# Inverse map of a mixture-of-experts layer: fp16 one-hots without tile-offset columns, each choice in its own PSUM columns

## The reference, cut to what matters

```python
x = hidden_states.reshape(-1, 256)                 # 2048 tokens
probs = softmax(x @ gate_w.T)                      # 64 experts
topk_w, topk_idx = top_k(probs, 6)
topk_w = topk_w / sum(topk_w)
h = silu(einsum('th,eih->tei', x, experts_w1))     # only the chosen experts count
y = einsum('tei,ehi->teh', h, experts_w2)
routed_out = sum over the 6 choices of topk_w * y[token, chosen expert]
out = layernorm(x + routed_out + shared_expert(x))
```

## Time and profile before

| | |
|---|---|
| median of 3 runs | 1412.85 us |
| the three runs | 1412.85, 1413.84, 1405.2 us |
| profiled execution, its own time | 1411.82 us |
| profiled execution, span from first to last instruction | 1410.1 us |
| mean granted TensorE clock | 0.894 |
| busy: PE, DVE, ACT, POOL | 1142.8, 874.5, 592.1, 568.6 us |

### The profile page before, as it was taken

One profiled execution on the slowest core, in us unless ns is written; L12 is line 12 of the kernel. 1 busy time (PEld: TensorE's weight loads), 2 busy tenths in 40 slices (PEclk: granted clock), 3 DMA queues, 4 the chain that ended last, 5 costly groups with the idle time before them and its releaser, 6 DMA issues. The chain is left out here.

```text
span 1410.1 us, 20915 instructions
## 1 busy us (share of the span) xinstructions
PE 1142.8 (81%) x6217; PEld 643.9 (46%) x6217; DVE 874.5 (62%) x1722; ACT 592.1 (42%) x1210; POOL 568.6 (40%) x565
## 2 busy tenths in 40 slices
PE   5599999999999778998898532869999889994673
PEld 2242222222222244665555431248888678882332
DVE  6499999999999366646455558943333222221656
ACT  1127777777777725450334200025555444430000
POOL 6001637765453737763110102544445754550000
PEclk9789999999999989999999755569999999997876
DMA  4970522441400130000000010058888888876411
GB/s 133 184 163 9 91 35 33 57 53 16 53 14 10 26 140 1 1 1 1 0 1 1 1 62 0 0 144 236 247 230 248 244 244 249 263 243 213 149 50 45
DMA packets 128366, 137.18 MB, mean 97 GB/s; under 512 B 47414, under 2 KB 99350, under 8 KB 128191
## 3 DMA queue, kind: packets, MB, share of 16 engines
q1 hardware_dynamic: 118767, 110.42, 31.7%
q0 software_dynamic: 9216, 25.18, 5.6%
q10 hardware_dynamic: 272, 0.26, 0.1%
HBM read 109.06 MB, written 24.12 MB: 94 GB/s over the span
## 5 line engine op out<-in xcount | busy, mean ns | idle before, releaser
L495 ACT ACTIVATE l_ret_store<-attn_st 128x512 f32<-128x512 f32 x512 | 280.1, 599 | 102.7 <-PE attn_st L406 92.8
L519 DVE TENSOR_REDUCE attn_neg<-attn_mx 128x8 f32<-128x1024 f32 x256 | 299.1, 1202 | 12.4 <-PE attn_mx L386 11.4
L1842 DVE SCALAR_TENSOR_TENSOR exp_sums<-exp_y_ps,moe_mask,exp_sums 128x256 f32 x159 | 77.0, 484 | 210.0 <-PE exp_y_ps L1776 101.6
L1767 PE MATMUL exp_h_ps<-exp_xt,exp_w 128*88 128x128 f32 x1272 | 169.8, 277 | 10.7 <-DMA exp_w<-in_w 9.7
L406 PE MATMUL attn_st<-attn_q_st,attn_k_st 128*128 128x512 bf16 x512 | 173.9, 384 | 3.0 <-ACT l_ret_store L495 2.1
L386 PE MATMUL attn_mx<-attn_k_st,attn_q_st 96*128 96x512 bf16 x512 | 155.8, 386 | 14.4 <-DVE attn_neg L519 13.9
L1776 PE MATMUL exp_y_ps<-exp_w,exp_ht 96*128 96x256 f32 x636 | 163.4, 379 | 0.0
L1767 PEld LDWEIGHTS exp_h_ps<-exp_xt,exp_w 128*88 128x88 f32 x1272 | 147.5, 158 | 29.0 <-DMA exp_w<-in_w 25.1
L418 PE MATMUL attn_o<-l_ret_store,l_ret_tab 128*32 128x512 f32 x1024 | 136.4, 605 | 0.8 <-ACT l_ret_store L495 0.8
L1726 POOL DMA_INDIRECT exp_rows<-x_rows,moe_tok_i x96 | 91.6, 954 | 90.3 <-PE exp_xt_ps L1756 68.1
L1731 POOL DMA_INDIRECT y_rows<-exp_sums,moe_dst_i x96 | 93.6, 975 | 81.2 <-DVE exp_sums L1842 73.0
(11 more groups left out here) (266 smaller groups left out, 1839.1 us busy)
## 6 DMA issues: line engine op xcount, KB each, us to landing
exp_w<-in_w SPq DMA_DIRECT2D x318, 176.0 KB
comb_got<-y_rows SPq DMA_DIRECT2D x16, 768.0 KB, 5.9
parts<-l0b_front SPq DMA_DIRECT2D x32, 192.0 KB, 10.8
attn_k_st<-parts SPq DMA_DIRECT2D x48, 128.0 KB, 7.2
attn_q_st<-parts SPq DMA_DIRECT2D x48, 128.0 KB, 7.8
l_ret_tab<-in_tables SPq DMA_DIRECT2D x4, 1024.0 KB, 11.0
keep_x_t<-in_x_t SPq DMA_DIRECT2D x4, 512.0 KB
keep_x<-in_x SPq DMA_DIRECT2D x1, 2048.0 KB, 14.7
```

The costliest lines, as they stand in the source:

```text
L495: act.activation(probs[s % 2][:, h], st_ps[n % BANKS][:], ACT.Exp, scale=SCALE0).then_inc(exp_done, 1)
L519: dve.tensor_reduce(neg[m % 2][:, i], mx_ps[slot["score", n] % 2][:].rearrange("p (j k) -> p j k", k=P), AX.X, ALU.max, negate=True).then_ ...
L1767: mm = pe.matmul(h_ps[b % 2][0:HALF, j * P:(j + 1) * P], w1[n][:, k, j], xt[b % XB][:, 0, k], start=(k == 0), stop=(k == KT - 1))
L1842: dve.scalar_tensor_tensor(out=sums[:, bass.ds(at, 1)], in0=y_ps[b % 2][:, 0:E].unsqueeze(1), scalar=mask[:, b:b + 1], in1=sums[:, bass.ds ...
```

## The change

- The 96 pairs now have one `hot_high` each, over the 96 tiles and not the 160 steps, times the token's number plus one (`token`). It and `hot_low` are fp16 and not bf16.
- Each choice `k` sums into its own 96 columns: five in `m_ps` (cleared by a product with zeros, 480 columns), the sixth in `t_ps`.
- After the loop no turning is needed: the sum over the choices is the token, and which choice's columns are not zero gives `k`. The row of `y_rows` is now k * 2048 + token, where it was (t * 8 + k) * 128 + lane.
- `mask` no longer comes from the loop's result: ahead of the loop DVE works out the first and last slot of each step's expert in its tile (`bound`), spreads them over a diagonal (`spread`), PE broadcasts them (`b_ps`), and after the loop's last one-hot DVE compares them with the lane.
- Four more constants on POOL at the start of the block; `combine` reads `y_rows` by the new layout (a line of SP).

```diff
-Y_ROWS = NT * KPAD * P
+Y_ROWS = TOP * TOK
-        hot_low = sb("hot_low", [P, HOTS, P], BF16)
-        hot_high = sb("hot_high", [P, HOTS, 2, TILES], BF16)
+        hot_low = sb("hot_low", [P, HOTS, P], F16)
+        hot_high = sb("hot_high", [P, HOTS, FULL], F16)
...
+            ordered(pool.memset(ones_f[:], 1.0))
+            ordered(pool.memset(zeros[:], 0.0))
+            ordered(pool.iota(token[:], pattern=[[P, NT]], base=1, channel_multiplier=1, ...
+            ordered(pool.iota(k_rows[:], pattern=[[TOK, TOP - 1]], base=0, channel_multiplier=0, ...
...
+            pe.matmul(m_ps[:, 0:(TOP - 1) * FULL], zeros[:, 0:P], zeros[:], start=True, stop=False)
+            pe.wait_ge(spread_in, 1)
+            pe.matmul(b_ps[:, 0:2 * TILES], ones_f[:], spread[:].rearrange("p a q -> p (a q)"),
+                      start=True, stop=True).then_inc(bounded, 1)
             for n, (t, k) in enumerate(pairs):
                 pe.wait_ge(hot_in, n + 1)
                 if n % 2:
                     pe.wait_ge(hot_low_in, n // 2 + 1)
-                pe.matmul(m_ps[:, 0:2 * TILES], hot_low[:, n % HOTS],
-                          hot_high[:, n % HOTS].rearrange("p a j -> p (a j)"),
-                          start=(n == 0), stop=(n == len(pairs) - 1)).then_inc(hot_used, 1)
-
-            pe.wait_ge(coded, 1)
...
-            mm.then_inc(tiled, 1)
+                place_in = m_ps[:, k * FULL:(k + 1) * FULL] if k < TOP - 1 else t_ps[:, 2 * P:2 * P + FULL]
+                pe.matmul(place_in, hot_low[:, n % HOTS], hot_high[:, n % HOTS],
+                          start=(t == 0 and k == TOP - 1), stop=(t == NT - 1 and k >= TOP - 2)).then_inc(hot_used, 1)
...
-            for i in range(2):
-                chain(dve.tensor_scalar(of_tile[:, i], iota[0:TILES // 2, 0:FULL],
-                                        tile_f[0:TILES // 2, i:i + 1], None, ALU.is_equal))
+            chain(dve.tensor_tensor(size[:], t_ps[:, EXPERTS:2 * EXPERTS], base[:], ALU.subtract))
+            for j in range(2):
+                chain(dve.tensor_tensor(passed[:, j], past[:], size[:, j:j + EXPERTS - 1].unsqueeze(1)
+                                        .to_broadcast([P, 2, EXPERTS - 1]), ALU.mult))
+            chain(dve.tensor_reduce(bound[:], passed[:], AX.X, ALU.add))
+            chain(dve.tensor_scalar(bound[:, 1], bound[:, 1], size[:, 0:1], None, ALU.add))
+            chain(dve.scalar_tensor_tensor(out=bound[:], in0=tile_f[:].unsqueeze(1).to_broadcast([P, 2, 2]),
+                                           scalar=float(-P), in1=bound[:], op0=ALU.mult, op1=ALU.add))
+            dve.tensor_tensor(spread[:], ident[0:TILES // 2, 0:TILES // 2].unsqueeze(1)
...
             for n, (t, k) in enumerate(pairs):
...
                 if n % 2 == 0:
                     dve.tensor_scalar(hot_low[:, n % HOTS], iota[:, 0:P], low[:, t, k:k + 1], None, ALU.is_equal)
-                dve.tensor_scalar(hot_high[:, n % HOTS, 0], iota[:], high[:, t, k:k + 1], float(t * KPAD + k + 1),
-                                  ALU.is_equal, ALU.mult)
-                dve.tensor_scalar(hot_high[:, n % HOTS, 1], iota[:], high[:, t, k:k + 1], lane[:, 0:1],
+                dve.tensor_scalar(hot_high[:, n % HOTS], iota[:, 0:FULL], high[:, t, k:k + 1], token[:, t:t + 1],
                                   ALU.is_equal, ALU.mult).then_inc(hot_in, 1)
+            dve.wait_ge(bounded, 1)
+            low_end, high_end = (b_ps[:, j * TILES:(j + 1) * TILES].rearrange("p (i q) -> p q i", i=2) for j in range(2))
+            chain(dve.tensor_scalar(above[:].rearrange("p (q i) -> p q i", i=2), low_end, lane[:, 0:1], None, ALU.is_le))
+            dve.scalar_tensor_tensor(out=mask[:].rearrange("p (q i) -> p q i", i=2), in0=high_end, scalar=lane[:, 0:1],
...
             dve.wait_ge(hot_used, len(pairs))
...
+            chain(dve.tensor_reduce(first_k[:], most.rearrange("p k j -> p j k"), AX.X, ALU.add))
+            chain(dve.scalar_tensor_tensor(out=tok_f[:], in0=first_k[:], scalar=-1.0, in1=last, op0=ALU.add, op1=ALU.add))
+            dve.tensor_copy(tok_i[:], tok_f[:]).then_inc(tok_in, 1)
+            chain(dve.scalar_tensor_tensor(out=k_at[:, 0:TOP - 1], in0=most, scalar=0.0,
+                                           in1=k_rows[:].unsqueeze(2).to_broadcast([P, TOP - 1, FULL]),
+                                           op0=ALU.is_gt, op1=ALU.mult))
+            chain(dve.tensor_scalar(k_at[:, TOP - 1], last, 0.0, float((TOP - 1) * TOK), ALU.is_gt, ALU.mult))
+            chain(dve.tensor_reduce(k_sum[:], k_at[:].rearrange("p k j -> p j k"), AX.X, ALU.add))
+            chain(dve.tensor_tensor(dst_i[:], k_sum[:], tok_f[:], ALU.add))
```

More of the change, by code:

```diff
@@ L1447, in route @@
         lane = sb("lane", [P, 1])
+        token = sb("token", [P, NT])
+        ones_f = sb("ones_f", [TILES // 2, P])
+        k_rows = sb("k_rows", [P, TOP - 1])
+        zeros = sb("zeros", [P, (TOP - 1) * FULL], F16)
         tile_no = sb("tile_no", [P, 2])
@@ L1464, in route @@
         HOTS = 16
-        hot_low = sb("hot_low", [P, HOTS, P], BF16)
-        hot_high = sb("hot_high", [P, HOTS, 2, TILES], BF16)
-        part = sb("part", [P, TILES])
-        code = sb("code", [P, TILES])
+        hot_low = sb("hot_low", [P, HOTS, P], F16)
+        hot_high = sb("hot_high", [P, HOTS, FULL], F16)
+        first_k = sb("first_k", [P, FULL])
+        tok_f = sb("tok_f", [P, FULL])
+        k_at = sb("k_at", [P, TOP, FULL])
+        k_sum = sb("k_sum", [P, FULL])
+        size = sb("size", [P, EXPERTS])
+        passed = sb("passed", [P, 2, 2, EXPERTS - 1])
+        bound = sb("bound", [P, 2, 2])
+        spread = sb("spread", [TILES // 2, 4, TILES // 2])
+        above = sb("above", [P, TILES])
         turns = sb("turns", [P, 2])
-        code_t = sb("code_t", [TILES // 2, 2, P])
-        of_tile = sb("of_tile", [TILES // 2, 2, FULL])
-        code_i, tok_hi = sb("code_i", [P, FULL], I32), sb("tok_hi", [P, FULL], I32)
         past = sb("past", [P, 2, EXPERTS - 1])
@@ L1478, in route @@
         t_ps = ps("t")
+        b_ps = ps("b")
         w_r_in, x_out = sem("w_r_in"), sem("x_out")
@@ L1519, in _ @@
             ordered(pool.memset(ones[:], 1.0))
+            ordered(pool.memset(ones_f[:], 1.0))
+            ordered(pool.memset(zeros[:], 0.0))
+            ordered(pool.iota(token[:], pattern=[[P, NT]], base=1, channel_multiplier=1,
+                              allow_small_or_imprecise_dtypes=True))
+            ordered(pool.iota(k_rows[:], pattern=[[TOK, TOP - 1]], base=0, channel_multiplier=0,
+                              allow_small_or_imprecise_dtypes=True))
             ordered(pool.memset(before[:], 1.0))
@@ new lines, in _ @@
+            dve.wait_ge(hot_used, len(pairs))
+            most = m_ps[:, 0:(TOP - 1) * FULL].rearrange("p (k j) -> p k j", k=TOP - 1)
+            last = t_ps[:, 2 * P:2 * P + FULL]
+            chain(dve.tensor_reduce(first_k[:], most.rearrange("p k j -> p j k"), AX.X, ALU.add))
[4 more added lines that the diff above has]
+                                           op0=ALU.is_gt, op1=ALU.mult))
@@ L1877, in _ @@
                     sp.wait_ge(added, (t - B + 1) * TOP)
-                sp.dma_start(got[t % B][:], a["y_rows"].rearrange("(t k p) n -> t p k n", k=KPAD, p=P)[t][:, 0:TOP]
+                sp.dma_start(got[t % B][:], a["y_rows"].rearrange("(k t p) n -> t p k n", k=TOP, p=P)[t]
                              ).then_inc(got_in[t % B], 16)
```

34 lines of the change are left out of this document (9 added, 25 removed).

## The result

| | before | changed |
|---|---|---|
| median | 1410.87 us (4 runs, 1405.2 to 1413.84) | 1387.7 us (4 runs, 1383.08 to 1390.0) |
| ratio, 95% interval | | 0.9844, 0.9816 to 0.9873 |
| profiled execution, span | 1410.1 us | 1386.2 us |

The forecast was 1394.5 us in a range of 1387 to 1405. The change is 1.6% faster, in the direction forecast and by more than forecast: 23.2 us between the medians for 17.3. (The median of before here has one run more than the one shown ahead of the prediction.)

What follows compares the result with a forecast made beforehand. DVE's instruction count was taken to bound the loop: 48.8 us to 31.2 (-17.6), +1.6 ahead, -1.3 behind, sum -17.3 us. From the profiled 1411.82 us that gave 1394.5 us, range 1387 to 1405.

Steps and rivals of the forecast that it cites:

- The instruction's own price: Loop: one `hot_low` at 0.16 us and two `hot_high` at 0.215 make an undisturbed DVE round of 0.59 to 0.60.
- The fp16 doubt: Loop: no row exists for fp16 with a bf16 iota as input; the forecast took the same price as bf16.
- The rival that had fp16 dearer: Loop: DVE leaves the fast mode (40.5 us) or POOL's fp16 one-hot becomes the bound (42); 1404 to 1405 us, chance 0.16.
- POOL's share: Loop: each POOL instruction beside DVE adds 0.05 us to a round, making it 0.65 us.
- POOL alone: Loop's start before the change: 13 POOL instructions in 8.15 us, 0.627 us each, taken as POOL's own pace.
- just short: Loop: POOL needs 48 x 0.627 = 30.1 us of the 31.2, so it is nearly but not the bound.
- If POOL and DVE could not overlap: Loop: the slower rival, rounds of 1.20 us and a loop of 57.6; time 1421 us, chance 0.05.
- Ahead and behind: Around the loop: seven chained DVE instructions for two ahead cost 1.6 us; the shorter map behind gains 1.3 us.
- reduce of 576 0.79: Behind the loop, in the map: DVE's last reduce, of `k_at`, 576 elements, priced at 0.79 us.
- What the sum takes as free: `experts` and `combine`: `combine`'s reads 2048 rows apart instead of 128, and scatters to new rows, cost nothing.
- the give-back rival: Later blocks: wider distance in `y_rows` costs 2 us, or TensorE's clock rises later, 2.5 us; 1397 to 1400, chance 0.10.
- The prediction's low case: Whole run: POOL hardly disturbs and the run falls to the scatter's low end; 1385 to 1391 us, chance 0.07.

Runs made afterwards that it cites:

- no_pool: Changed kernel with DVE making all 96 `hot_low` and POOL none in the loop; loop 36.0 us, for 31.0 in the changed kernel.
- bf16_low: Changed kernel with `hot_low` in bf16 instead of fp16, `hot_high` still fp16; loop 30.9 us, POOL's median 667 ns.
- cols160: Changed kernel with 160 columns in each `hot_high`, of which PE takes 96; loop 29.9 us, 0.625 us a round.
- cols128: Changed kernel with 128 columns in each `hot_high`, of which PE takes 96; loop 29.3 us, 0.610 us a round.
- three_engines: Changed kernel with the 96 `hot_low` shared out: DVE 24, POOL 36, ACT 36; loop 27.1 us, ratio to the kernel before 0.9862.
- layout_only: Kernel before with only the new layout of `y_rows`, its old loop kept; ratio to the kernel before 1.0010.
- old_layout: Changed kernel with the old layout of `y_rows`, two more small DVE instructions; 1413.29 us, ratio to the kernel before 0.9876.
- before_again: Kernel before, unchanged, run once more on the second chip; ratio 0.9989, loop 48.6 us.

## Why the prediction was right

**The direction, the place and the size of the gain in `route`: right.** The loop was DVE's, and what it lost the kernel lost. Up to DVE's next free start 31.2 us were forecast and 31.22 came; the profiles of the changed kernel on the second chip have the same loop within 0.1 us.

**The instruction's own price: right.** Reading starts and not lengths gave 0.59 to 0.60 for a round, where no_pool's starts give 0.591. The forecast length of 0.29 us for a `hot_high` shows only without POOL (300 ns); with it they are 337 ns in the mean.

**The fp16 doubt: settled.** The prediction took the same price as bf16. bf16_low shows no difference on POOL, and the fp16 `hot_high` of 160 columns in cols160 (0.231 us to the next start) has the bf16 price of the earlier trace rows, 0.23. The rival that had fp16 dearer, 1404 to 1405 us, did not come, in neither of its two forms.

**POOL's share: right in the sum, not in the rule.** The 0.05 us for each POOL instruction was carried over as a constant. With 96 columns it was 0.06; cols128 and cols160 show next to zero. It is luck that the case forecast was close to the old price. The 0.627 us called "POOL alone" was not alone either: DVE was busy all the time beside those 13 instructions, and three_engines has 0.595 for the same instruction. The bound "just short" by that figure was never tested; what came is that POOL and DVE were both busy all through the loop. If POOL and DVE could not overlap, the loop would have taken 57.6 us; it took 31.2. The Trainium skill (SBUF — State Buffer, Who interferes with whom) states that DVE in a two-port mode and GpSimd exclude one another for a whole instruction. No trace names the mode; if these one-hots run in a two-port one, the rule does not hold here for the whole instruction. That DVE loses time beside POOL at all agrees with it: a `hot_high` is 300 ns long without POOL and 337 with it. POOL's instruction, of which no row without DVE exists, has 626 ns beside the old loop (the first 17) and 669 beside the new one.

**Ahead and behind: right but for one term.** +1.56 for +1.6, and -1.15 for -1.3. The failed term is "reduce of 576 0.79": it took 1.12 and, with the gap, 1.15, because of the distance of its reads. The other steps came out shorter by some hundredths each.

**What the sum takes as free: right about the mechanism, silent about the scatter.** `combine`'s reads by the new layout, which the give-back rival priced at 2 us, cost nothing that a run shows (layout_only, old_layout). The clock's rise came some 9 us behind the first product of `experts`, as before:

```profile
913.00:918.00 5.00, 2.04 (x6) 0.86 (x6) 1.17 (x4) 2.05 (x6) 3.78 (x5) 0.50 0.64 186
918.00:923.00 5.00, 4.27 (x19) 3.88 (x20) 0.00 (x0) 2.17 (x4) 3.78 (x5) 0.52 0.91 264
923.00:928.00 5.00, 5.00 (x36) 4.53 (x35) 1.51 (x4) 2.96 (x8) 3.78 (x5) 1.00 0.95 283
```

The first transposes start at 913.9 us here and at 931.3 before, and the clock goes from 0.50 to 1.00 at about 923 and 940.

**The measured gain was larger than the forecast one.** 23.2 us between the medians, ratio 0.9844 with an interval up to 0.9873, where 17.3 us would have been 0.9877. On the second chip the ratio was 0.9872 and 0.9867, that is 18 to 19 us, and 17.3 of 1430 us, 0.9879, lies inside both intervals. In the two profiled executions of the first chip the rest lies behind the first gather, 5.2 us in `experts` and 1.3 in `combine`. On the second chip the runs rule out the layout as its cause; that `experts` scatters by up to 8 us on one chip between executions of kernels that differ only in `route` (358.4 to 366.1 in the profiles here) makes chance enough of a reason, but that it was chance on the first chip is inferred and not shown. The prediction's low case, "the run falls to the low end of the scatter", is the closest to what came; it should have had more than 0.07, since the three runs of before already differed by 8.6 us.

## What to carry to other kernels

Where many short instructions stand one behind another on an engine, count instructions and read their starts: one `hot_high` a pair instead of two was worth 18.7 us (48.6 us in before_again, 29.9 in cols160), and 64 columns less in each made the loop 1.1 us longer. Take such prices from a stretch where no other engine works beside them, and the disturbed price from another stretch, but don't carry the difference over as a constant to a denser loop. And before a gain of a per cent is read as the change's, look at how the stages that it doesn't touch differ between the two profiles.

## What the hardware showed that was not expected

- Longer instructions made a shorter loop: 96 columns in 31.0 us, 160 in 29.9, 128 in 29.3, each beside the same work on POOL.
- A DVE reduce over 576 f32 numbers took 753 ns with its groups of six side by side and 1121 ns with the six 384 bytes apart in SBUF; the one over 480 numbers 384 bytes apart in PSUM took 0.65 us, no more than its count. Writing 480 numbers 24 bytes apart took 0.99 us for 0.65.
- With 96 columns, POOL's instruction cost DVE its 0.06 us in one instruction of three: the first `hot_high` of a round took 0.272 us to the next start, the second 0.214.
- The same kernels were 1.3 to 1.8% slower on what their times say is a second chip, all of it in one block, with stretches in which PE, DMA and the granted clock all fell together, 0.66 of the clock and 138 GB/s in the lowest 10 us.
